# Statistics between VectorE's two maxima of a step, loads behind the maxima's transfers, k rotated at 28, and the high part of the maxima on ScalarE

## The reference

```python
def _layernorm(x, axis=-1, eps=1e-05):
    m = jnp.mean(x, axis=axis, keepdims=True)
    v = jnp.var(x, axis=axis, keepdims=True)
    return (x - m) / jnp.sqrt(v + eps)

def attn(x, Wq, Wk, Wv, Wo):                      # H = 16, G = 4, hd = 16, Hkv = 4
    q, k, v = x @ Wq, x @ Wk, x @ Wv
    k = jnp.repeat(k.reshape(B, S, Hkv, hd), G, axis=2)
    v = jnp.repeat(v.reshape(B, S, Hkv, hd), G, axis=2)
    ...
    q, k = _rope(q, cos, sin), _rope(k, cosk, sink)
    ...
    scores = jnp.einsum('bhqd,bhkd->bhqk', q, k) / jnp.sqrt(jnp.float32(D))
    p = jax.nn.softmax(scores, axis=-1)
    o = jnp.einsum('bhqk,bhkd->bhqd', p, v)
    return o.transpose(0, 2, 1, 3).reshape(B, S, D) @ Wo

def ffn(input, weight, alpha, bias):              # ternary_quantize gives -1, 0 or 1
    return jnp.einsum('bsd,od->bso', input, ternary_quantize(weight) * alpha) + bias

x = x + _layernorm(attn(_layernorm(x), Wq, Wk, Wv, Wo))
x = x + _layernorm(ffn(_layernorm(x), weight, alpha, bias))
```

## Time and profile before

| | |
|---|---|
| median of 3 runs | 1544.8 us (1543.61 to 1551.56) |
| profiled execution, its own time | 1535.35 us |
| its span | 1533.2 us |
| PE busy | 1438.2 us (94%) |
| VectorE busy | 1348.5 us (88%) |
| ScalarE busy | 1238.7 us (81%) |
| POOL busy | 752.6 us (49%) |
| granted TensorE clock, mean | 0.979 |

### The profile page before, as it was taken

How to read it: one execution, slowest core, us unless ns; L and a number is a source line. 1 busy time by engine, 2 the same in 40 slices (tenths; PEclk the granted TensorE clock), 3 DMA queues, 4 the chain that set the end, 5 groups by cost and what they waited for, 6 DMA issues and landing times.

```text
span 1533.2 us, 32212 instructions
## 1 busy us (share of the span) xinstructions
PE 1438.2 (94%) x12350; PEld 462.2 (30%) x12350; DVE 1348.5 (88%) x1535; ACT 1238.7 (81%) x2419; POOL 752.6 (49%) x1206
## 2 busy tenths in 40 slices
PE   5789999999999999999999999999999999999996
PEld 5122322223222322223222232223223232222236
DVE  5789999899989999899998999899998989999914
ACT  2078888888988888898888889888888888989881
POOL 4322075545656355663755546562556545363240
PEclk9589999999999999999999999999999999999999
DMA  3411121311222121221213112221211212120001
GB/s 112 112 25 57 36 55 40 95 33 49 68 72 57 41 73 28 74 75 45 55 40 94 34 49 68 72 57 41 74 30 44 74 45 62 42 63 30 29 18 48
DMA packets 72921, 84.92 MB, mean 55 GB/s; under 512 B 17632, under 2 KB 58464, under 8 KB 71328
## 3 DMA queue, kind: packets, MB, share of 16 engines
q1 hardware_dynamic: 71952, 82.08, 19.0%
q10 hardware_dynamic: 816, 0.79, 0.2%
HBM read 46.66 MB, written 24.64 MB: 47 GB/s over the span
## 4 chain that ended last, share of the span: by engine, by line
PE 59%; DVE 22%; issue 7%; ACT 6%; DMA 3%; POOL 2%; SPq 0%; POOLq 0%; ACTq 0%; DVEq 0%
PE smax L978 22%; PE pv L1000 20%; DVE row_max L1221 17%; ACT probs L879 4%; PE ring L1113 4%; PE ring L1024 3%; PE ring L1087 3%; PE ring L1121 2%; DMA q_rows<-max_rows 2%; DVE sy_bn L1201 1%; PE ring L1048 1%; PE ring L1101 1%; PE ring L1107 1%; DVE max_parts L1239 1%; DVE sa_bn L1201 1%
## 5 line engine op out<-in xcount | busy, mean ns | idle before, releaser
L1221 DVE TENSOR_REDUCE row_max<-smax 128x1 f32<-128x1024 f32 x1024 | 1197.7, 1215 | 111.5 <-PE smax L978 105.0
L879 ACT ACTIVATE probs<-ring 128x512 f32<-128x512 f32 x2048 | 1102.6, 596 | 153.2 <-PE ring L1024 135.3
L978 PE MATMUL smax<-k_rows,q_rows 48*128 48x512 f16 x2048 | 632.2, 389 | 43.6 <-DVE row_max L1221 34.8
L1024 PE MATMUL ring<-q_rows,k_rows 50*128 50x512 f16 x2048 | 635.7, 384 | 9.5 <-DMA q_rows<-max_rows 8.1
L1000 PE MATMUL pv<-probs,v_cols 128*32 128x256 f32 (+1 forms) x6520 | 611.2, 447 | 4.3 <-ACT heads L934 3.9
L978 PEld LDWEIGHTS smax<-k_rows,q_rows 48*128 48x128 f16 x2048 | 117.8, 94 | 535.1 <-issue 266.7
L1000 PEld LDWEIGHTS pv<-probs,v_cols 128*32 128x32 f32 x6520 | 128.8, 108 | 324.9 <-issue 189.6
L1024 PEld LDWEIGHTS ring<-q_rows,k_rows 50*128 50x128 f16 x2048 | 132.4, 93 | 59.5 <-ACT probs L879 41.4
L572 POOL TENSOR_TENSOR attnT<-pairs,inv_rows 128x512 f32<-128x512 f32 x31 | 39.3, 1269 | 206.0 <-DMA inv_rows<-inv_sums_dram 206.0
L551 POOL TENSOR_TENSOR act<-act,bias_sb 128x256 f32<-128x256 f32 x60 | 42.4, 726 | 106.7 <-ACT act L923 106.7
L1113 PE MATMUL ring<-wo_sb,attnT 128*128 128x256 f32 x256 | 71.3, 403 | 6.1 <-POOL attnT L572 2.2
(11 more groups left out here) (167 smaller groups left out, 1152.6 us busy)
## 6 DMA issues: line engine op xcount, KB each, us to landing
q_stage_dram<-q_parts SPq DMA_DIRECT2D x45, 256.0 KB, 2.5
q_rows<-q_stage_dram SPq DMA_DIRECT2D x30, 384.0 KB, 5.5
x_in<-in_L_attn_x SPq DMA_DIRECT2D x8, 1024.0 KB, 6.2
pairs<-heads SPq DMA_DIRECT2D x64, 128.0 KB
inv_rows<-inv_sums_dram SPq DMA_DIRECT2D x32, 256.0 KB
res<-in_L_attn_x SPq DMA_DIRECT2D x16, 512.0 KB, 4.4
out<-res SPq DMA_DIRECT2D x15, 512.0 KB, 3.2
k_rows<-k_stage_dram SPq DMA_DIRECT2D x64, 96.0 KB, 3.3
```

Of the source, the lines that this page charges most:

```text
L879: eng.activation(probs[:, s % PSLOTS, j, :], ring[:, n % RING, :], ACT.Exp, scale=score_unit).then_inc(ring_read, 1)
L978: mm = eng.matmul(smax[:, side, c, :], q_rows[at:to, qc, kv * KVP + jp, qt * P:(qt + 1) * P], k_rows[at:to, kv, c * 512:(c + 1) * 512], st ...
L1024: eng.matmul(ring[:, n % RING, :], k_rows[at:to, g, kt * P:(kt + 1) * P], q_rows[at:to, h.qc, g * KVP + j // 2, :], start=True, stop=True)\
L1221: eng.tensor_reduce(row_max[:, g % 2, at:at + 1], smax[:, side, :, :].rearrange("p c n -> p (c n)"), AX.X, ALU.max).then_inc(max_read, 1)
```

## The change

Five things are done, all by tables and by the place of calls:

- **Loads.** x_in is loaded at 6 instead of 5, so behind the maxima's transfer of step 5, and res at 10 instead of 6 (both for even halves; res for odd ones too).
- **Jobs.** XT at 2 to 5 instead of 0 to 3, V at 5, 6, 7 and 16 instead of 0 to 3, Q at 15 instead of 16, K at 16 instead of 6; in half 0 XT at 13 and 14 instead of 11 and 12, K and Q two and more steps later. A_NORM is 12 instead of 13.
- **k.** Swapped at 22, rotated at 28 (behind the bias), staged at 31, instead of 18, 18 and 23. POOL takes two groups of V at 19 and one at 27.
- **Statistics.** `statistics` puts up to `ROOM` of a step's `bn_stats` between its two maxima, by the kind of the step's job, and the rest behind. x statistics are at 5 to 8 instead of 0 to 3, a at 9, 10, 11, 11, y at 15, 15, 16, 16.
- **Split.** The high float16 part is made by ScalarE (`high_max`) in the step after the last unit, ahead of its third exponential; VectorE makes the low part alone, behind both maxima of that step (4, 12, 20, 28). The operand of zeros is gone.

```diff
-PRO_EARLY = {11: [("XT", 0, 0), ("XT", 1, 0)], 12: [("XT", 0, 1), ("XT", 1, 1)], 17: [("K",)],
-             19: [("Q", 0, 0)], 21: [("Q", 0, 1)]}
-PRO = {0: [("XT", 0, 0)], 1: [("XT", 1, 0)], 2: [("XT", 0, 1)], 3: [("XT", 1, 1)],
-       6: [("K",)], 16: [("Q", 0, 0)], 30: [("Q", 0, 1)]}
-
-PRO1 = {0: [("V", 0)], 1: [("V", 1)], 2: [("V", 2)], 3: [("V", 3)],
-        16: [("Q", 1, 0)], 30: [("Q", 1, 1)]}
+PRO_EARLY = {13: [("XT", 0, 0), ("XT", 1, 0)], 14: [("XT", 0, 1), ("XT", 1, 1)], 19: [("K",)],
+             21: [("Q", 0, 0)], 24: [("Q", 0, 1)]}
+PRO = {2: [("XT", 0, 0)], 3: [("XT", 1, 0)], 4: [("XT", 0, 1)], 5: [("XT", 1, 1)],
+       15: [("Q", 0, 0)], 16: [("K",)], 30: [("Q", 0, 1)]}
+
+PRO1 = {5: [("V", 0)], 6: [("V", 1)], 7: [("V", 2)], 16: [("V", 3)],
+        15: [("Q", 1, 0)], 30: [("Q", 1, 1)]}
...
-X_MOM_FIRST, X_MOM = (0, 1, 2, 5, 6, 7, 8, 8), (0, 0, 1, 1, 2, 2, 3, 3)
-A_MOM, Y_MOM, F_MOM = (9, 10, 11, 12), (16, 16, 16, 16), (27, 27, 30, 30)
+X_MOM_FIRST, X_MOM = (0, 1, 2, 3, 4, 5, 6, 7), (5, 5, 6, 6, 7, 7, 8, 8)
+A_MOM, Y_MOM, F_MOM = (9, 10, 11, 11), (15, 15, 16, 16), (27, 27, 30, 30)
 
 
 INVERT, SCALED = {22: 0, 4: -1}, {27: 0, 7: -1}
 
-X_NORM_FIRST, X_NORM, A_NORM, Y_NORM, F_NORM = 9, 18, 13, 17, 31
+X_NORM_FIRST, X_NORM, A_NORM, Y_NORM, F_NORM = 8, 18, 12, 17, 31
 ACT_SPLIT, BIAS = {21: 0, 23: 1}, {26: (0, 1), 28: (2, 3)}
-X_LOAD_FIRST, X_LOAD, STORE, RES_LOAD = 13, 5, 3, 6
-K_ROT, Q_ROT_FIRST, Q_ROT = 18, 22, 8
-K_SWAP = 18
-K_STAGE = 23
+X_LOAD_FIRST, X_LOAD, STORE, RES_LOAD = 15, 6, 3, 10
+K_ROT, Q_ROT_FIRST, Q_ROT = 28, 22, 8
+K_SWAP = 22
+K_STAGE = 31
 Q_STAGE, Q_LOAD, Q_LOAD_FIRST = 14, 16, 6
+V_TAKEN = {19: (0, 1), 27: (2,)}
+ROOM = {"Q": 2, "K": 2, "V": 1, "WO": 1, "FF": 1}
 XT_JOBS = ((0, 0), (1, 0), (0, 1), (1, 1))
-X_SPLIT_FIRST, X_SPLIT = {13: (0, 1, 2, 3)}, {1: (0,), 2: (1,), 3: (2,), 4: (3,)}
+X_SPLIT_FIRST, X_SPLIT = {15: (0, 1, 2, 3)}, {3: (0,), 4: (1,), 5: (2,), 6: (3,)}
...
+    def between_units(self, s):
+
+        return max((ROOM.get(job[0], 0) for job in self.jobs_behind(s, 1)), default=0)
+
...
-                if s == K_ROT:
-                    rotate_k(eng, h)
-                    split_k(eng, h.pro, rot_out[:, 0, :])
...
+            if h.pro is not None and s == K_ROT:
+                rotate_k(eng, h)
+                split_k(eng, h.pro, rot_out[:, 0, :])
...
-                    if h.scores and h.qc == 1 and s % KT == 3 and s > KT and h.b is not LAST:
-                        g = s // KT - 1
-                        eng.wait_ge(pv_step, (h.group0 + g + 1) * KT)
-                        take_v(h, h.b + 1, g)
+                    if h.scores and h.qc == 1 and s in V_TAKEN and h.b is not LAST:
+                        eng.wait_ge(ring_read, h.done("V", 3))
+                        for g in V_TAKEN[s]:
+                            eng.wait_ge(pv_step, (h.group0 + g + 1) * KT)
...
+                        if i == 2 and (s + LEAD) % KT == 0 and h.first < s <= h.maxima:
+                            high_max(h, (s + LEAD) // KT - 1)
...
+            def high_max(h, g):
+
+                nth, par = h.group0 + g, g % 2
+                eng.wait_ge(max_read, (nth + 1) * G * ST)
+                if h.scores:
+                    eng.wait_ge(ring_full, h.done("MT", g - 3) if g >= 3 else h.base)
+                rows = row_max[:, par, :].rearrange("p (r n) -> p r n", r=2)
+                eng.activation(max_parts[:, par, :, 0, :], rows, ACT.Copy, scale=1.0 / ROW_UNIT).then_inc(max_split, 1)
...
+            def due(s, when, first, last):
+
+                at = when.index(s) if s in when else 0
+                return range(at + min(first, when.count(s)), at + min(last, when.count(s)))
+            def statistics(h, s, first, last):
+
+                if h.mom is not None:
+                    for t in due(s, h.x_mom, first, last):
+                        if t == 0:
+                            eng.wait_ge(x_loaded, (h.mom + 1) * 16)
+                            eng.wait_ge(x_norm, RAISED + h.mom * (KT + 1))
+                        eng.bn_stats(st_x[0][:, t, :], x_in[:, t, :]).then_inc(x_mom, 1)
+                if h.epi is None:
+                    return
+                nth = h.epi[0] * 2 + h.epi[1]
+                for t in due(s, A_MOM, first, last):
+                    if t == 0:
+                        eng.wait_ge(a_norm, RAISED + nth * (ST + 1))
+                    eng.wait_ge(ring_read, h.done("WO", t, 1))
+                    eng.bn_stats(st_a[0][:, t, :], act[:, t, :]).then_inc(a_mom, 1)
...
-                eng.wait_ge(max_read, (nth + 1) * G * ST)
-
-                if h.scores:
-                    eng.wait_ge(ring_full, h.done("MT", g - 3) if g >= 3 else h.base)
-                m1, m2 = max_parts[:, par, :, 0, :], max_parts[:, par, :, 1, :]
+                eng.wait_ge(max_split, nth * 2 + 1)
                 rows = row_max[:, par, :].rearrange("p (r n) -> p r n", r=2)
-                eng.scalar_tensor_tensor(m1, rows, 1.0 / ROW_UNIT, zeros[:, :, :], ALU.mult, ALU.add).then_inc(max_split, 1)
-                eng.wait_ge(max_split, nth * 2 + 1)
-                eng.scalar_tensor_tensor(m2, rows, 1.0 / ROW_UNIT, m1, ALU.mult, ALU.subtract).then_inc(max_split, 1)
+                eng.scalar_tensor_tensor(max_parts[:, par, :, 1, :], rows, 1.0 / ROW_UNIT, max_parts[:, par, :, 0, :],
+                                         ALU.mult, ALU.subtract).then_inc(max_split, 1)
 
             def half(h):
-                if h.epi is not None:
-                    nth_epi = h.epi[0] * 2 + h.epi[1]
                 for s in h.steps:
                     g, part = (s + LEAD) // KT, (s + LEAD) % KT
+                    room = h.between_units(s)
                     if s < h.maxima:
                         if part == 0:
 
                             at_least(eng, max_split, (h.group0 + g - 1) * 2)
                         reduce_max(h, g, 2 * part)
+                        statistics(h, s, 0, room)
                         reduce_max(h, g, 2 * part + 1)
-                        if part == KT - 1:
-                            split_max(h, g)
+                        if part == 0 and s > h.first:
+                            split_max(h, g - 1)
+                    else:
+                        statistics(h, s, 0, room)
+                        if s == h.maxima and s > h.first:
+                            split_max(h, g - 1)
                     if s in INVERT and (h.scores if INVERT[s] >= 0 else h.flush):
                         invert(h, INVERT[s])
-                    if h.mom is not None:
-                        if now := due(s, h.x_mom):
-                            if now[0] == 0:
-                                eng.wait_ge(x_loaded, (h.mom + 1) * 16)
-                                eng.wait_ge(x_norm, RAISED + h.mom * (KT + 1))
-                            moments(x_in, st_x, x_mom, *now)
-                    if h.pro is not None and h.alone:
+                    if h.alone and h.epi is not None:
...
```

55 lines of the change are left out of this document (22 added, 33 removed).

## The result

| | before | after |
|---|---|---|
| median (runs) | 1544.2 us (4, 1538.71 to 1551.56) | 1491.6 us (4, 1490.47 to 1492.92) |
| ratio | | 0.966, 95% interval 0.9615 to 0.9698 |
| profiled execution | 1535.35 us | 1492.92 us |
| its mean granted clock | 0.979 | 0.978 |

Between the two profiled executions the difference is 42.4 us, close to the sum of 39.7. So the sum was about right in total (not in each term), and what failed is the step from the profiled execution to the median: "which lies 9.4 above it".

A forecast was written before the change was run, and what follows sets the result against it. PE and VectorE almost level, so time is PE's work plus its waits. Terms summed to 39.7, so 40 us: profiled execution 1495.3, median 1544.8 - 40 = 1505 us; range 1496 to 1526, own range 1496 to 1514 at 0.66.

The forecast's parts named there:

- which lies 9.4 above it: Last move of the forecast: the median of the runs lies 9.4 us above the profiled execution, before and after.
- Loads: Even halves: with loads behind the maxima's transfers, five PE waits in halves 2 to 10 go, 6.9 us.
- k rotated at 28: Step 20, even halves: the rotation leaves, so four PE waits of 1.4 to 1.6 us go, 6.2 us.
- High and low part: Plain steps run at 2.20 instead of 2.27 us, 5 us gained; ScalarE's inserts at steps 12 and 28 cost 1.5.
- Statistics: Step 17: statistics between the maxima at 15 and 16 take back 8.0 of 9.5 us of PE waits.
- x statistics: Step 4: moved to steps 5 to 8 with one between the maxima, they give 1.0 of 1.9 us.
- Half 0: XT moved from step 11 to 13 covers PE's 4.36 us wait for POOL's normalisation: 4.4 us gained.
- V jobs: Moved to steps 5 to 7, they lengthen the time before WO's first job: 3.0 of 4.1 us gained.
- Step 31: Six PE waits of 0.17 us there go with XT's move, 0.9 us.
- the rival without the statistics: Engines too level for the statistics to fit: 19.8 us of terms vanish, 20.5 stay, 1524 us; chance 0.09.
- The low part does meet POOL: Rival: low part delayed by POOL at step 28 in even halves and by the root at 12; 1516 us, chance 0.17.
- The margin at 28: Step 28: the low part is issued at 2.6 us, 0.25 before POOL's third instruction, so it escapes delay.

## Why the prediction was right or wrong

**What bounds the kernel**: right. The list of PE's waits named every place that moved.

**Offset of the median, the failed step.** It took the 9.4 us between profiled execution and median as a constant that the change would leave alone, and no term of its sum had the clock in it. They are falls of the clock behind PE's longer waits, on the maxima's transfer and on VectorE at step 20, which come in one execution and not in the next; the profiled execution by chance had only one short fall after half 0. From half 1 on, seven waits on the transfer and three of 1.6 us at step 20 were left to chance in each run before; now there are two on the transfer and none at step 20. At the changed kernel's clock of 0.979 the kernel before would take 1503 / 0.979 = 1535 us: of the 53 us, 44 are fewer waits and shorter work, and 9 to 10 the clock.

**Loads** (6.9): the waits went as said. The term left out the falls behind them; loads are worth 19 to 20 us by themselves. By the products of time and clock (1502.9 and 1494.8, medians) some 8 of the 19.0 are there whatever the clock, and some 11 are the clock.

**k rotated at 28** (6.2): wrong. The collisions of step 20 were real, but it was the split's move that ended their waits. Alone, k gains nothing on one kernel, costs 6.6 us on another, in whose one trace the clock falls behind step 28 in four halves, and undone it changes nothing.

**High and low part** (5 for the pace, less 1.5 for ScalarE): mis-sized, 23.4 us alone and 14.4 undone. Step 28 went whole (7.8 where 5.8 was taken), and step 13 (3.75) where nothing was. ScalarE's price was right: 64 instructions of 221 ns, between the ends of 0 and 0.6 us, without a wait on the maxima in the timed halves. The 1.5 us charged for it show nowhere: the waits on `pv` stay at 3.9 us when it is added, and PE's waits for ScalarE's ring slots at 1.0. Its group in the changed kernel (busy us, mean ns | idle before):

```profile
L899 ACT ACTIVATE max_parts<-row_max 128x16 f16<-128x16 f32 x64 | 14.1, 221 | 25.2 <-DVE row_max L1267 25.2
```

(The 25.2 us are one wait, for the first maxima of all.)

**Statistics** (8.0 at step 17): the waits shrank by 8.3, but 4.7 of that is back as waits on `pv` one step later, so the term is worth about 3.6. The reason given, room between the maxima, adds nothing where it stands now; whether the spreading, the room or the jobs' new steps did it is open.

**x statistics** (1.0): step 4's six waits of 0.31 us are gone, 1.9; the high part's move alone turned them into five of 0.2 at step 5. **Half 0** (4.4): the wait went as said, and the lower clock for 3.5 us behind it with it, which the term left out. **V jobs** (3.0): 2.0 gained at WO, but 2.4 are the new waits on `pv` at step 2 of the odd halves. **Step 31** (0.9): nothing; the six waits of 0.17 us are unchanged, so XT did not cause them.

**The rivals.** The sum of 20.5 for the rival without the statistics leaves out step 31's 0.9 and ScalarE's 1.5; with them it is 19.9, which changes nothing. The low part does meet POOL in even halves, at steps 4 and 20 for 1.04 us and at 28 for 0.26, and in halves 13 to 15 at step 20, but no wait of PE follows in any of them. The margin at 28 held as put. At step 12 the root and the low part overlap in 15 halves without delay. Timeline of POOL, half 7:

```profile
714.07 1.04 POOL L414 TENSOR_TENSOR sa_rs<-sa_ve,m_half 128x4 f32<-128x4 f32 x1
```

VectorE beside it:

```profile
714.25 0.17 DVE L1281 SCALAR_TENSOR_TENSOR max_parts<-row_max,max_parts 128x16 f16<-128x16 f32 x1
```

POOL in half 8, step 20, with a full-width instruction:

```profile
821.20 1.16 POOL L550 TENSOR_TENSOR act_parts<-actT,act_parts 128x512 f16<-128x512 f32 x1
```

VectorE there, held to its end:

```profile
821.35 1.04 DVE L1281 SCALAR_TENSOR_TENSOR max_parts<-row_max,max_parts 128x16 f16<-128x16 f32 x1
```

The Trainium skill (GPSIMD Engine Reference, Key points) makes no difference between POOL's instructions in this contention; these rows do.

## What to carry to other kernels

When the runs of a kernel scatter more than its edits are worth, multiply each time by its mean granted clock before arguing from one trace: if the product is constant, the profiled execution may lack what the median pays. In this kernel a wait of TensorE, on a transfer or on VectorE, could cost its length again in a lower clock behind it, so look at the clock behind every wait over 1 us, and put a small transfer on the critical path ahead of the large ones in its queue. And an edit of five parts should be priced part by part on the chip: here two parts carried three quarters of it, and two, among them the one it was named after, nothing. Undoing one part at a time doesn't tell which of two parts that can stand in for each other did the work.
